# Group 0 tiled by whole batches, its first tile made from the first gather alone, and w1 loaded at once

## The chip, the cores and the metric

The kernel runs on one core of a Trainium2 chip. The core has a matrix engine (PE, with its weight loads PEld), a vector engine (DVE), a scalar engine (ACT), GpSimd (POOL) and a queue engine (SP) that here issues DMAs; 16 DMA engines move data between HBM and the on-chip memory SBUF. The metric is the device time of one launch in microseconds, the median of several runs.

## The reference

For 512 rows of a batch, 32 ids each pick a row of 32 numbers from 32 tables. Two layers of a compressed interaction network follow, then a small dense tower.

```python
e = jnp.stack([tbl_0[ids[:, 0]], ..., tbl_31[ids[:, 31]]], axis=1)   # 512 x 32 fields x 32
x0 = prev = e
for W in (filter_0, filter_1):                                       # 1024 x 128, then 4096 x 128
    z = jnp.einsum('bhd,bmd->bhmd', x0, prev).reshape(b, h * m, d)
    prev = jax.nn.relu(jnp.einsum('bpd,pn->bnd', z, W[0]))
    outs.append(prev)
z = jnp.sum(jnp.concatenate(outs, axis=1), axis=-1)                  # sum over d
h = jnp.concatenate([z, dense_ctx], axis=1)
h = jnp.maximum(h @ W_top1 + b_top1, 0.0)
h = jnp.maximum(h @ W_top2 + b_top2, 0.0)
y = h @ W_top3
```

## The kernel before

**Tiling.** The 512 x 32 pairs of batch and d are 16,384 columns: 32 groups of 512 columns (16 batches), each group four tiles of 128 (u = 0 to 3). Layer 0 is made for a whole group. Layer 1 is made tile by tile: the tile's c (128 maps of layer 0 by 128 columns) is the stationary operand, and w1 streams past it in eight banks (k = 0 to 7) of four fields, 512 columns each. Each bank is three matmuls, because numbers are split into a high and a low part (`hi` by `w_hi`, `hi` by `w_lo`, `lo` by `w_hi`; lines 915, 916 and 923), and goes to one of six PSUM banks in a ring, so bank k of a tile reuses the place of the one six banks earlier.

**Behind PE.** ACT multiplies banks 0, 1, 3, 5, 6 by the embedding value (L571), DVE banks 2, 4, 7 and adds them to ACT's (L740), POOL folds one half of the tile's products onto the other (L441), and DVE reduces the rest in two halves (L752). Those engines follow PE in an order written out by hand: functions are called at places (u, k) of the loop in `body`.

**Groups.** Three gathers of embeddings are made ahead. POOL issues four gathers per group (one for each four batches). SP writes the gathered rows to a scratch in HBM (`send`) and reads them back as pairs (`fetch`), POOL multiplies them to z (L431), ACT rounds z (L532), and PE's layer 0 of the next group stands between layer-1 banks at the places `Z_USED_AT`.

**The start**, which the change rewrites. Group 0 does not go through the scratch. Its gathered rows are spread over 512 columns (each block of 32 rows copied to its own quarter, zeros elsewhere: `spread_hi` on ACT, `spread_lo` on DVE), and six pairs of matmuls with 0/1 matrices ("picks", L940 and L943) put the rows that belong together under each other, one result for the first factor and five for the second (`PICK_ORDER` 4, 0, 1, 2, 3). ACT copies the first factor out, DVE multiplies: first for the first tile alone, then for the other three (`multiply_others`). PE makes layer 0 of the first tile, then layer 1 of the first tile with layer 0 of the other three (`other_tiles`) between its banks; layer 1 of the tile u = 1 comes behind that. Group 0 is laid out like all others: its columns run over (batch, o, d within o), and tile o takes 8 of the 32 values of d of all 16 batches. So every tile needs all four gathers.

PE runs warm-up matmuls on zeros until its inputs arrive (`WARM_UP`). POOL issues twelve gathers (three groups), the last four behind `first_c_hi`, and then takes the low parts of w1's banks 6 and 7. DVE takes the low parts of the others (`rest_w1`), ACT rounds all (`round_w1`). SP loads w1 in four parts of 512 KB: the first at once, the second and third when group 0's gathers are in, the fourth behind the sending of group 1:

```python
            filters(0)
            ...
            sp.wait_ge(gathered[0], 16 * TG)
            for n in range(1, W1_LOADS - 1):
                filters(n)
            ...
            send(Group(0, 1))
            filters(W1_LOADS - 1)
            fetch(Group(0, 1))
```

## Time and profile before

| | us |
|---|---|
| median of 3 runs (834.12 to 834.23) | 834.16 |
| the profiled execution | 833.78 |
| its span, first to last instruction | 832.0 |
| PE busy in it | 825.9 |
| DVE, ACT, POOL busy | 789.3, 795.8, 731.0 |
| granted clock of PE | 1.00 throughout |

The profile is one execution. A row of a timeline gives the start and the length from it in us, the engine, the line of the kernel, the operation, what it writes and reads with shapes, and how many were merged into the row; in brackets stands the idle time of the engine before it and what ended that. Matmuls are pipelined and their ends are modelled: a 512-column matmul lasts 0.39 in the rows, but the next one starts 0.23 later. An fp32 matmul counts as two.

### The profile page before, as it was taken

How to read it: one execution, taken by the hardware profiler on the slowest of the kernel's cores; microseconds unless marked ns; L12 is line 12 of the kernel's file. 1: busy time of each engine (PE TensorE's matmuls, PEld its weight loads, DVE VectorE, ACT ScalarE, POOL GpSimd, SP SyncE). 2: the span in 40 equal slices, each digit the busy share in tenths (PEclk: the TensorE clock that was granted, in tenths of full speed). 3: DMA queues.
4: the chain of work that ended last, by engine and by line, in shares of the span. 5: the costliest groups of instructions: out<-in, count | busy, mean ns of one | idle time of the engine just before them, and what ended most of it. 6: DMA issues, size and time to landing. Idle time of an engine off the chain costs nothing.

```text
span 832.0 us, 15690 instructions
## 1 busy us (share of the span) xinstructions
PE 825.9 (99%) x3627; PEld 677.7 (81%) x3627; DVE 789.3 (95%) x2061; ACT 795.8 (96%) x2808; POOL 731.0 (88%) x550
## 2 busy tenths in 40 slices
PE   8999999999999999999999999999999999999999
PEld 6688888888888888888888888888888888888887
DVE  7799999999999999999999999999999999999996
ACT  4799999999999999999999999999999999999995
POOL 5898999989999999999999999999999999999860
PEclk9999999999999999999999999999999999999999
DMA  5541222221233221132331132221122222122000
GB/s 149 180 143 32 66 81 85 86 85 36 63 82 84 84 86 47 51 85 82 84 87 49 48 87 80 84 86 55 43 87 80 86 85 68 33 83 78 1 13 2
DMA packets 62024, 60.91 MB, mean 73 GB/s; under 512 B 26059, under 2 KB 36939, under 8 KB 61934
## 3 DMA queue, kind: packets, MB, share of 16 engines
q1 hardware_dynamic: 57838, 57.80, 23.4%
q0 software_dynamic: 4096, 2.11, 1.6%
q8 instruction: 32, 0.52, 0.3%
q14 instruction: 58, 0.48, 0.2%
HBM read 55.51 MB, written 4.31 MB: 72 GB/s over the span
## 4 chain that ended last, share of the span: by engine, by line
PE 97%; DMA 1%; POOL 1%; issue 0%; SPq 0%; DVE 0%; ACT 0%
PE ps_y L915 28%; PE ps_y L923 28%; PE ps_y L916 28%; PE ps_c L898 3%; PE ps_c L897 3%; PE ps_c L896 3%; POOL gat L452 1%; PE ps_c L894 1%; DMA w_raw<-w 1%; PE ps_c L885 0%; DMA gat<-table,rows 0%; PE ps_y L1019 0%; DMA ids_and_bounds_sb<-ids_and_bounds 0%; POOL w_lo L459 0%; PE ps_y L1021 0%
## 5 line engine op out<-in xcount | busy, mean ns | idle before, releaser
L571 ACT ACTIVATE prod<-ps_y,es 128x128 f32<-128x128 f32 x2560 | 754.1, 647 | 15.8 <-PE ps_y L923 15.6
L740 DVE SCALAR_TENSOR_TENSOR prod<-ps_y,es,prod 128x128 f32<-128x128 f32 x1536 | 422.6, 340 | 28.7 <-PE ps_y L923 26.4
L915 PE MATMUL ps_y<-w_hi,c_both 128*128 128x512 f32 x1024 | 402.8, 393 | 1.0 <-POOL w_lo L459 1.0
L923 PE MATMUL ps_y<-w_hi,c_both 128*128 128x512 f32 x1024 | 398.8, 390 | 0.0
L916 PE MATMUL ps_y<-w_lo,c_both 128*128 128x512 f32 x1024 | 398.6, 389 | 0.0
L441 POOL TENSOR_TENSOR prod<-prod 128x768 f32<-128x768 f32 x128 | 247.1, 1931 | 45.9 <-DVE prod L740 34.2
L752 DVE TENSOR_REDUCE csum<-prod 128x64 f32<-128x896 f32 x256 | 276.5, 1081 | 0.1
L916 PEld LDWEIGHTS ps_y<-w_lo,c_both 128*128 128x128 f32 x1024 | 192.4, 188 | 43.2 <-issue 1.0
L915 PEld LDWEIGHTS ps_y<-w_hi,c_both 128*128 128x128 f32 x1024 | 192.5, 188 | 42.9 <-issue 2.8
L923 PEld LDWEIGHTS ps_y<-w_hi,c_both 128*128 128x128 f32 x1024 | 192.2, 188 | 41.4
L431 POOL TENSOR_TENSOR z<-first,second 128x512 f32<-128x512 f32 x155 | 199.7, 1299 | 0.1
L419 POOL TENSOR_TENSOR z_lo<-z,z_hi 128x512 fp32r<-128x512 f32 x121 | 155.9, 1298 | 1.0 <-issue 1.0
L410 POOL DMA_INDIRECT gat<-table,rows_now x116 | 110.6, 953 | 31.3 <-issue 28.2
L532 ACT ACTIVATE z_hi<-z 128x512 fp32r<-128x512 f32 x120 | 109.3, 911 | 0.0
L898 PE MATMUL ps_c<-z_lo,w_hi 128*128 128x512 f32 x120 | 48.8, 407 | 0.0
L896 PE MATMUL ps_c<-z_hi,w_hi 128*128 128x512 f32 x120 | 46.6, 388 | 0.0
L897 PE MATMUL ps_c<-z_hi,w_lo 128*128 128x512 f32 x120 | 46.6, 388 | 0.0
L725 DVE TENSOR_REDUCE h<-c_both 128x16 f32<-128x1024 f32 x32 | 38.7, 1208 | 0.0
L532 ACT ACTIVATE z_hi<-z,copy_sb 128x512 fp32r<-128x512 f32 x31 | 35.8, 1154 | 0.0
L555 ACT ACTIVATE c_parts<-csum 128x512 f32<-128x512 f32 x31 | 33.8, 1090 | 0.0
L897 PEld LDWEIGHTS ps_c<-z_hi,w_lo 128*128 128x128 f32 x120 | 22.5, 188 | 4.7
L896 PEld LDWEIGHTS ps_c<-z_hi,w_hi 128*128 128x128 f32 x120 | 22.5, 188 | 4.7
(122 smaller groups left out, 295.7 us busy)
## 6 DMA issues: line engine op xcount, KB each, us to landing
second<-et_scratch SPq DMA_DIRECT2D x155, 256.0 KB, 4.8
first<-et_scratch SPq DMA_DIRECT2D x31, 256.0 KB, 3.2
et_scratch<-gat SPq DMA_DIRECT2D x62, 64.0 KB
w_raw<-w SPq DMA_DIRECT2D x4, 512.0 KB, 4.7
h_scratch<-h_sums SPq DMA_DIRECT2D x120, 2.0 KB
gat<-table,rows_now POOLq DMA_INDIRECT x116, 2.4
wt_sb<-wt SPq DMA_DIRECT2D x2, 512.0 KB
rows_now<-rows SPq DMA_DIRECT2D x29, 2.0 KB, 1.7
```

The lines of the kernel that those rows point to most:

```text
L410: pool.indirect_dma_start(out=gat[:, g.r, u * D:(u + 1) * D], out_offset=None, in_=table, in_offset=bass.IndirectOffsetOnAxis(ap=rows_now[ ...
L419: nc.gpsimd.tensor_tensor(z_lo[:, k, :], z[:, k, :], z_hi[:, k, :].bitcast(F32), ALU.subtract).then_inc(z_lo_ready, LOWS if unsplit(g) else 1)
L431: nc.gpsimd.tensor_tensor(z[:, k, :], first[:, :], second[:, k, :], ALU.mult).then_inc(z_ready, 1)
L441: nc.gpsimd.tensor_tensor(high, high, low, ALU.add).then_inc(folded, 1)
L532: nc.scalar.activation(z_hi[:, k, :], z[:, k, :], ACT.Copy, scale=copy_sb[:, 0:1] if k == LASTK else 1.0).then_inc(z_hi_ready, splits_at_o ...
L571: last = nc.scalar.activation(prod[:, buffer_of(g, u), place // 2, :, place % 2], ps_y[:, bank_of(g, u, k), j * N:(j + 1) * N], ACT.Copy, ...
L740: last = nc.vector.scalar_tensor_tensor(out=summed, in0=ps_y[:, bank_of(g, u, k), j * N:(j + 1) * N], scalar=es[:, g.r, u, h:h + 1], in1=s ...
L752: nc.vector.tensor_reduce(csum[:, g.r, maps, u], prod[:, buffer_of(g, u), fields_folded(g, u) // 2:SCALED // 2, maps, :].rearrange("p a n ...
L896: nc.tensor.matmul(ps_c[:, :], w0_hi[:, k, :], high, start=(k == 0), stop=False)
L915: nc.tensor.matmul(out, hi, w_hi, start=True, stop=False)
L916: nc.tensor.matmul(out, hi, w_lo, start=False, stop=False)
L923: nc.tensor.matmul(out, lo, w_hi, start=False, stop=True).then_inc(y_ready, 1)
```

## The change

Group 0 gets its own column order: tile u holds four whole batches by 32 of d, and these are the rows that gather u brings. The first gather has a semaphore of its own (`first_gathered`), and the first tile is made from it alone.

- The spread is made by DVE, by multiplying the gathered rows with a 0/1 table (`own_block`, four more columns of `copy_sb`), so two memsets of 512 columns and the eight small copies go. The first tile's six picks are single fp32 matmuls of 128 columns on unrounded data; those of the other tiles are twelve matmuls of 384 columns and stand between the layer-1 banks of the first tile (`pick_others`), in two free banks and `ps_h1`.
- The other tiles' layer 0 comes between banks 4 to 7 of the first tile, not 0 to 5.
- SP issues all four w1 loads at once. POOL takes the low parts of three banks, not two, and issues the last four of its first twelve gathers behind them. The warm-up is 22 matmuls instead of 32.
- The rest of w0 moves to (1, 0). Layer 0 of group 1 moves one bank later, its Relu and rest two banks. The sum of group 0's layer 1 over d is made tile by tile in group 1 (`sum_first`: four transposes and four reductions in place of a reduction, a transpose and a reduction).

```diff
-WARM_UP = 32
+WARM_UP = 22
 PICK_ORDER = (4, 0, 1, 2, 3)
+PICK_LOADS = ("first",) + PICK_ORDER
+OTHER_PICKS = {"first": 4, 4: 5, 0: None, 1: 4, 2: 5, 3: None}
+LATE_LO = 3
...
-            filters(0)
+            for n in range(W1_LOADS):
+                filters(n)
-            sp.wait_ge(gathered[0], 16 * TG)
-            for n in range(1, W1_LOADS - 1):
-                filters(n)
...
-            filters(W1_LOADS - 1)
...
+                ).then_inc(gathered[n // TG] if n else first_gathered, 16)
+            pool.wait_ge(rows_step, 4)
+            for n in range(2 * TG):
+                gather_first(n)
+            for k in range(NK - LATE_LO, NK):
                                         ALU.subtract).then_inc(w1_last_lo, 1)
+            for n in range(2 * TG, FIRST_ROWS):
+                gather_first(n)
...
-            round_w1((0, 1))
-            act.wait_ge(spread_zeroed, 2)
-            act.wait_ge(gathered[0], 16 * TG)
-            for q in range(BT):
-                at = slice(q * F, (q + 1) * F)
-                nc.scalar.activation(spread_hi[at, q * P:(q + 1) * P], gat[at, 0, :], ACT.Copy).then_inc(spread_hi_ready, 1)
+            round_w1((0,))
             act.wait_ge(picked, 1)
-            nc.scalar.activation(first_picked, ps_y[:, PICKS["first"], :], ACT.Copy).then_inc(first_copied, 1)
-            round_z(slice(0, 1), first_z_hi, 1)
-            round_w1((2, 3))
+            round_z(FIRST_TILE, first_z_hi, 1)
+            round_w1((1,))
             act.wait_ge(l0_first, 1)
             rectify_first(FIRST_TILE, ps_h1, first_c_hi)
-            round_w1((4, 5))
+            round_w1((2,))
+            act.wait_ge(spread_ready, 2)
+            nc.scalar.activation(spread_hi, spread[:, OTHER_TILES], ACT.Copy).then_inc(spread_hi_ready, 1)
+            round_w1((3, 4))
+            nc.scalar.activation(first_picked[:, OTHER_TILES], picks_of_others("first"), ACT.Copy).then_inc(first_copied, 1)
+            round_w1((5,))
             def body(g, number):
                 more = number is None or number + 1 < GROUPS
                 for u in range(TG):
                     for k in range(NK):
+                        if number == 0 and (u, k) == (0, 1):
+                            act.wait_ge(z_ready, 1)
+                            round_z(OTHER_TILES, z_hi_ready, SPLIT)
+                            round_w1((6,))
                         if number == 0 and (u, k) == (0, 3):
-                        if number == 0 and (u, k) == (0, 5):
+                            round_w1((7,))
+                        if number == 0 and (u, k) == (0, 6):
...
-            nc.vector.tensor_tensor(w0_lo[:, 0:LASTK, :], w0_sum[:, 0:LASTK, :], w0_hi[:, 0:LASTK, :].bitcast(F32),
-                                    ALU.subtract).then_inc(w_ready, 1)
+            def spread_first():
+                dve.wait_ge(first_gathered, 16)
+                shape = [P, BT, D]
+                nc.vector.tensor_tensor(spread[:, FIRST_TILE].rearrange("p (q d) -> p q d", d=D),
+                                        gat[:, 0, 0:D].unsqueeze(1).broadcast_to(shape), own_block.unsqueeze(2).broadcast_to(shape),
+                                        ALU.mult).then_inc(spread_ready, 1)
+                nc.vector.transpose(es[:, 0, 0, :], gat[:, 0, 0:D]).then_inc(first_es, 1)
+                dve.wait_ge(gathered[0], rows_gathered(Group(0, 0)))
+                shape = [P, TG - 1, BT, D]
+                nc.vector.tensor_tensor(spread[:, OTHER_TILES].rearrange("p (u q d) -> p u q d", q=BT, d=D),
+                                        gat[:, 0, D:TG * D].rearrange("p (u d) -> p u d", d=D).unsqueeze(2).broadcast_to(shape),
+                                        own_block.unsqueeze(1).unsqueeze(3).broadcast_to(shape), ALU.mult).then_inc(spread_ready, 1)
...
+                dve.wait_ge(picked, len(PICK_LOADS) + 2 + PICK_ORDER.index(k))
+                multiply_picked(k, OTHER_TILES, picks_of_others(k), z_ready)
...
+            def sum_first():
+                dve.wait_ge(parts_rectified, 1)
+                dve.wait_ge(h1_written[0], 16 * BT)
+                for u in range(TG):
+                    if u > 0:
+                    nc.vector.transpose(c1_turned[:, :], c1_parts[:, :, u]).then_inc(c1_ready if u == TG - 1 else first_turned, 1)
+                    nc.vector.tensor_reduce(h1_sums[:, 0, :].rearrange("p (j b) -> p j b", b=BT)[:, :, u],
+                                            c1_turned[:, :].rearrange("p (j d) -> p j d", d=D), AX.X,
+                                            ALU.add).then_inc(h1_summed if u == TG - 1 else first_turned, 1)
...
-            rest_w1(0)
-            rest_w1(1)
-            for q in range(BT):
-                dve.wait_ge(spread_hi_ready, q + 1)
+            spread_first()
+                multiply_picked(k, FIRST_TILE, ps_y[:, PICKS[k], FIRST_TILE], first_z)
+            rest_z(FIRST_TILE, first_z_lo, 1)
+            rest_w1(0)
+            rest_first(FIRST_TILE, ps_h1, first_c_hi, first_c_lo)
+            rest_w1(1)
+            spread_others()
+            rest_w1(2)
+            dve.wait_ge(spread_hi_ready, 1)
+            nc.vector.tensor_tensor(spread_lo, spread[:, OTHER_TILES], spread_hi.bitcast(F32), ALU.subtract).then_inc(spread_lo_ready, 1)
+            rest_w1(3)
+            turn_others()
+            dve.wait_ge(first_copied, 2)
+            multiply_others(LASTK)
             multiply_others(0)
-            turn(Group(0, 0))
-            rest_first(FIRST_TILE, ps_h1, first_c_hi, first_c_lo)
+            rest_w1(4)
             multiply_others(1)
-            rest_w1(2)
-            multiply_others(2)
-            rest_w1(3)
-            multiply_others(3)
-            multiply_others(LASTK)
                         if number == 0 and (u, k) == (0, 2):
-                            rest_w1(4)
-                        if number == 0 and (u, k) == (0, 4):
-                            rest_w1(5)
+                            multiply_others(2)
+                            multiply_others(3)
                             dve.wait_ge(z_hi_ready, SPLIT)
-                            dve.wait_ge(z_ready, KP)
-                            rest_z(slice(1, TG), z_lo_ready, LOWS)
+                            dve.wait_ge(z_ready, 1)
+                            rest_z(OTHER_TILES, z_lo_ready, LOWS)
+                        if number == 0 and (u, k) == (1, 0):
+                            rest_w0()
...
+                        if more and (u, k) == ((3, 5) if number == 0 else (3, 3)):
...
+                    if k < NK - LATE_LO:
+                        pe.wait_ge(w1_last_lo, k + 1 + LATE_LO - NK)
+                    if k in (4, 5):
+                        pe.wait_ge(z_ready, k - 1)
...
-            pe.wait_ge(picks_ready, 1)
-            pe.wait_ge(spread_hi_ready, BT)
                 table_of, shift = {"first": (1, 0), LASTK: (1, P // 2)}.get(load) or (0, 16 * load)
-                out, picks_of = ps_y[:, PICKS[load], :], picks_r[:, table_of, shift:shift + P]
-                nc.tensor.matmul(out, picks_of, spread_hi, start=True, stop=False)
+            pe.wait_ge(spread_ready, 1)
+            for load in PICK_LOADS:
+                table_of, at = picks_at(load)
+                nc.tensor.matmul(ps_y[:, PICKS[load], FIRST_TILE], picks_sb[:, table_of, at], spread[:, FIRST_TILE],
+                                 start=True, stop=True).then_inc(picked, 1)
+            def pick_others(load):
-                nc.tensor.matmul(out, picks_of, spread_lo, start=False, stop=True).then_inc(picked, 1)
-            def first_layer0(k, tiles, out):
+                    pe.wait_ge(picks_ready, 1)
+                    pe.wait_ge(spread_hi_ready, 1)
+                    pe.wait_ge(spread_lo_ready, 1)
+                if load == 1:
+                    pe.wait_ge(first_copied, 2)
+                if load in (2, 3):
+                    pe.wait_ge(z_ready, load - 1)
+                table_of, at = picks_at(load)
+                nc.tensor.matmul(picks_of_others(load), picks_r[:, table_of, at], spread_hi, start=True, stop=False)
+                nc.tensor.matmul(picks_of_others(load), picks_r[:, table_of, at], spread_lo, start=False, stop=True).then_inc(picked, 1)
-                return first_layer0(k, slice(1, TG), ps_c[:, OTHER_TILES])
-            pe.wait_ge(w_ready, 2)
+                if k < LASTK:
+                    pe.wait_ge(z_ready, PICK_ORDER.index(k) + 1)
+                    return nc.tensor.matmul(ps_c[:, OTHER_TILES], w0_sum[:, k, :], z[:, k, OTHER_TILES], start=(k == 0), stop=False)
...
-            other_tiles(0)
-            Z_USED_AT_FIRST = ((1, 6), (2, 1), (2, 4), (2, 6), (3, 0))
+            Z_USED_AT_FIRST = ((1, 7), (2, 2), (2, 5), (2, 7), (3, 1))
...
-                        if number == 0 and u == 0 and 1 <= k < LASTK:
-                            other_tiles(k)
-                        if (number, u, k) == (0, 0, LASTK):
+                        if number == 0 and u == 0 and k in (2, 3):
+                            for load in PICK_LOADS[3 * k - 6:3 * k - 3]:
+                                pick_others(load)
+                        if number == 0 and u == 0 and k in (4, 5):
+                            other_tiles(k - 4)
+                        if number == 0 and u == 0 and k == 6:
+                            other_tiles(2)
+                            other_tiles(3)
                             other_tiles(LASTK).then_inc(l0_done, 1)
```

At its start PE had, from the last pick through layer 0 of the first tile to layer 1:

```order
L940 MATMUL ps_y<-z_hi,picks_r 128x512
L943 MATMUL ps_y<-z_lo,picks_r 128x512
L949 MATMUL ps_h<-z,w_sum 128x128 x4
L951 MATMUL ps_h<-z_lo,w_lo 128x128
L949 MATMUL ps_c<-z,w_sum 128x384
L915 MATMUL ps_y<-w_hi,c_both 128x512
L916 MATMUL ps_y<-w_lo,c_both 128x512
```

It now has, from the warm-up on to the third bank and the first picks of the other tiles:

```order
L1001 MATMUL ps_y<-z_lo 128x512 x22
L1011 MATMUL ps_y<-csum,picks_sb 128x128 x6
L1032 MATMUL ps_h<-z,w_sum 128x128 x4
L1034 MATMUL ps_h<-z_lo,w_lo 128x128
L982 MATMUL ps_y<-w_hi,c_both 128x512
L983 MATMUL ps_y<-w_lo,c_both 128x512
L982 MATMUL ps_y<-w_hi,c_both 128x512
L983 MATMUL ps_y<-w_lo,c_both 128x512
L990 MATMUL ps_y<-w_hi,c_both 128x512 x2
L982 MATMUL ps_y<-w_hi,c_both 128x512
L983 MATMUL ps_y<-w_lo,c_both 128x512
L990 MATMUL ps_y<-w_hi,c_both 128x512
L1025 MATMUL ps_y<-z_hi,picks_r 128x384
L1026 MATMUL ps_y<-z_lo,picks_r 128x384
```

The picks of the first tile are narrow, and those of the others have moved behind the third layer-1 bank.

SP's queue at the start, before (`w_raw<-w` are the w1 loads, `et_scratch<-gat` the sending of group 1):

```order
L318 DMA copy_sb<-copy_of 128x2
L319 DMA picks_sb<-picks 128x384
L314 DMA w_raw<-w 128x1024 x3
L340 DMA et_scratch<-gat 4x32x128 x2
L314 DMA w_raw<-w 128x1024
L357 DMA first<-et_scratch 128x1x512
```

and now:

```order
L331 DMA copy_sb<-copy_of 128x6
L332 DMA picks_sb<-picks 128x384
L327 DMA w_raw<-w 128x1024 x4
L351 DMA et_scratch<-gat 4x32x128 x2
L368 DMA first<-et_scratch 128x1x512
```

The fourth load has moved ahead of the sending, and the wait for group 0's gathers that stood within the first three is gone.

POOL's start before (`gat<-table` are gathers, `w_lo` the low parts of w1, `z` the products of group 1, `prod` the fold):

```order
L452 DMA gat<-table,rows 128x32 x12
L459 ISA
L459 TENSOR_TENSOR w_lo<-w_raw,w_hi 128x512 x2
L431 TENSOR_TENSOR z<-first,second 128x512 x3
L441 TENSOR_TENSOR prod<-prod 128x768
```

and now:

```order
L460 DMA gat<-table,rows 128x32 x8
L471 ISA
L471 TENSOR_TENSOR w_lo<-w_raw,w_hi 128x512 x3
L460 DMA gat<-table,rows 128x32 x4
L441 TENSOR_TENSOR z<-first,second 128x512 x3
L451 TENSOR_TENSOR prod<-prod 128x768
```

Four gathers have moved behind the low parts of w1, which are three.

## Rows read from the trace of the kernel before

**Rows 1.** The page: busy time and share of each engine.

```profile
PE 825.9 (99%) x3627; PEld 677.7 (81%) x3627; DVE 789.3 (95%) x2061; ACT 795.8 (96%) x2808; POOL 731.0 (88%) x550
```

**Rows 2.** Timeline of PE, the first 27 us: start, length, what.

```profile
1.45 9.00 PE L934 MATMUL ps_y<-z_lo 128*128 128x512 f32 x32 [1.45 <-DVE z_lo L655]
...
12.08 0.47 PE L940 MATMUL ps_y<-z_hi,picks_r 128*128 128x512 f32 x1 [1.63 <-ACT z_hi L590]
...
14.98 1.05 PE L949 MATMUL ps_h<-z,w_sum 128*128 128x128 f32 x8
...
15.79 0.31 PE L951 MATMUL ps_h<-z_lo,w_lo 128*128 128x128 f32 x1
...
16.64 0.69 PE L915 MATMUL ps_y<-w_hi,c_both 128*128 128x512 f32 x1
...
18.32 0.81 PE L949 MATMUL ps_c<-z,w_sum 128*128 128x384 f32 x2
...
19.20 0.40 PE L916 MATMUL ps_y<-w_lo,c_both 128*128 128x512 f32 x1
...
25.59 0.47 PE L915 MATMUL ps_y<-w_hi,c_both 128*128 128x512 f32 x1 [0.32 <-POOL w_lo L459]
...
26.36 0.40 PE L915 MATMUL ps_y<-w_hi,c_both 128*128 128x512 f32 x1
```

**Rows 3.** DMA to landing of gathers issued at 4.02, 5.48-9.45, 10.70-13.20, 37.97-41.74.

```profile
DMA to landing us min/median/max: 3.7/3.7/3.7
...
DMA to landing us min/median/max: 2.3/2.5/3.0
...
DMA to landing us min/median/max: 3.3/4.1/5.1
...
DMA to landing us min/median/max: 6.0/6.2/6.5
```

**Rows 4.** Timeline of DVE, and its busy time in one group's 25.4 us.

```profile
7.11 0.69 DVE L678 TENSOR_TENSOR w_lo<-w_sum,w_hi 128x512 fp32r<-128x512 f32 x1
...
7.72 0.35 DVE L681 SCALAR_TENSOR_TENSOR w_lo<-w_hi,copy_sb,w_sum 128x128 fp32r<-128x128 f32 x1
...
15.38 0.28 DVE L701 TENSOR_TENSOR z_lo<-z,z_hi 128x128 fp32r<-128x128 f32 x1
...
32.12 1.07 DVE L752 TENSOR_REDUCE csum<-prod 128x64 f32<-128x896 f32 x1
...
51.70:77.10 25.40, 25.40 (x114) 20.92 (x113) 24.41 (x64) 24.89 (x91) 23.11 (x18) 1.00 0.24 71
```

**Rows 5.** Timeline of ACT, the Relu of the first tile.

```profile
16.13 0.28 ACT L542 ACTIVATE c_both<-ps_h 128x128 fp32r<-128x128 f32 x1 [0.26 <-PE ps_h L951]
```

**Rows 6.** SP's issues; landing of the first w1 load; GB/s (last column), 14 to 15.

```profile
3.09 8.29 SPq L314 DMA_DIRECT2D w_raw<-w  x3
...
34.41 3.18 SPq L359 DMA_DIRECT2D second<-et_scratch  x5
...
39.19 0.39 SPq L371 DMA_DIRECT2D wt_sb<-wt  x1
...
DMA to landing us min/median/max: 5.0/5.0/5.0
...
14.00:15.00 1.00, 1.00 (x6) 0.78 (x6) 0.65 (x3) 0.55 (x2) 0.14 (x1) 1.00 1.00 406
```

**Rows 7.** Timeline of POOL: a gather, w1's low parts, products, the first fold.

```profile
19.17 0.94 POOL L452 DMA_INDIRECT gat<-table,rows  x1 [0.30 <-issue]
...
22.93 2.52 POOL L459 TENSOR_TENSOR w_lo<-w_raw,w_hi 128x512 fp32r<-128x512 f32 x2 [1.56 <-ACT w_hi L580]
...
25.60 3.80 POOL L431 TENSOR_TENSOR z<-first,second 128x512 f32<-128x512 f32 x3
...
29.36 1.85 POOL L441 TENSOR_TENSOR prod<-prod 128x768 f32<-128x768 f32 x1
```

**Rows 8.** Warm-up matmuls between 3 and 4 us: ns min/median/max, first and last start.

```profile
L934 PE MATMUL ps_y<-z_lo x4: 628/628/628, 2.5 to 3.8; 128*128 128x512 f32 x4
```

More of the change, by code:

```diff
@@ L564, in scale @@
                 if k == ACT_BANKS[u][0]:
-                    if u == 0:
+                    if u == 0 and g.times(1) == 0:
+                        act.wait_ge(first_es, 1)
+                    elif u == (1 if g.times(1) == 0 else 0):
                         act.wait_ge(es_ready, g.times(1, 1))
@@ L622, in body @@
                             rectify_end(u - 2)
-                        if more and (u, k) == (3, 1):
+                        if more and (u, k) == ((3, 3) if number == 0 else (3, 1)):
                             rectify_hi(g.plus(1))
@@ L732, in scale @@
                 if k == DVE_BANKS[u][0]:
-                    if u == 0:
+                    if u == 0 and g.times(1) == 0:
+                        dve.wait_ge(first_es, 1)
+                    elif u == (1 if g.times(1) == 0 else 0):
                         dve.wait_ge(es_ready, g.times(1, 1))
```

106 lines of the change are left out of this document (59 added, 47 removed).

## The prediction

> **What bounds the kernel now.** I read the page's busy line first: PE is busy for 825.9 us, 99% of the span [rows 1]. So a change pays only if PE starts its steady stream earlier, does less work, or waits less. I then read PE's timeline over the first 30 us [rows 2]. It has four pieces to see: the 32 warm-up matmuls from 1.45 (9.00 us), a gap of 1.6 until the first pick at 12.08, the twelve picks until layer 0 of the first tile at 14.98, and the first layer-1 matmul at 16.64. The second tile of group 0 (u = 1) starts at 26.36, and from there PE has no more gaps worth naming. That makes 26.36 the mark of this study. Everything behind it is a rigid block of PE work which the change hardly touches. What counts is the time at which u = 1 starts, and whether PE stays fed behind it.
>
> **What the change removes ahead of the mark.** Before, the picks wait for all four gathers; now one is enough. Call the landing of the first gather T0. In the trace of before it is issued at 4.02 and lands 3.7 later, at 7.7 [rows 3]. DVE has finished the part of w0 that the first tile needs by then: w_lo of 128 columns at 7.72 comes 0.6 earlier with the row of 0.69 ahead of it moved away, so it ends at 7.4 [rows 4]. The warm-up is no obstacle either: ten matmuls fewer at 0.23 each (the spacing, as between 25.59 and 26.36) end it at 10.45 − 2.3 = 8.2 [rows 2].
>
> **The chain from T0 to the first layer-1 matmul**, all from the durations of the nearest kind of instruction [rows 2, 4, 5]. The spread product (128x128 on DVE) 0.28, with the hand-over the first pick starts at T0+0.36. A 128-column fp32 matmul takes PE 0.27 (1.05 for four); the first result stands at T0+0.8, ACT's copy takes 0.28, to T0+1.1. The five products on DVE follow the picks at 0.27 each, the last ending at T0+2.5, its rest at T0+2.7 (0.28). The last layer-0 matmul adds 0.31 and its start-up (T0+3.1), the Relu 0.28 (T0+3.4). Layer 1 starts at T0+3.45. ACT's round of the last product and the w1 rests lie beside this.
>
> **From there to u = 1.** PE has 24 layer-1 matmuls at 0.23 = 5.5; 12 picks of 384 columns, at three quarters of that, 0.17 each = 2.0; four fp32 matmuls of 384 columns at 0.65 (18.32 to 19.20 less one of 0.23) = 2.6; the low one 0.2. That is 10.3. The picks of three tiles and one of the fp32 products are new in this stretch: before they stood ahead of 16.64. Waits that I find by laying the DVE rows in their new order: bank 1 waits 0.4 for its w1 rest, which now stands behind the rest of c (0.29 + 0.69 after the Relu); 0.2 ahead of bank 2, behind the spread of the others; 0.5 ahead of bank 4, which waits for the third product; 0.1 ahead of u = 1. Sum 1.2. So u = 1 starts at T0 + 3.45 + 10.3 + 1.2 = T0 + 15.0 (rounded). The waits for the last w1 rests (0.32 ahead of the last bank is one of them [rows 2]) go, because w1 is all in by then. Against 26.36, **the gain is 11.4 − T0**. All steps hang on T0 alone (ACT and DVE reach their w1 work only behind the first tile), so a late T0 moves the whole chain.
>
> **T0 is the term that decides.** Now SP issues all four w1 loads at 3.09, 3.5, 4.0 and 4.4, around the issue of the first gather (4.02 to 5.17). The trace shows what a gather does behind such a backlog. With little ahead of them gathers land 2.3 to 3.0 after their issue. The three issued from 10.70, just when the second and third w1 load were issued, took up to 5.1 [rows 3]; the four issued from 37.97, with a fetch (five loads of it from 34.41) and the tower's weights (39.19) queued on SP [rows 6], took 6.0 to 6.5 [rows 3]. So gathers stand behind what SP has queued, even those parts issued a little later. By these rows T0 is: 7.7 if the three added loads do not matter; 4.02 + 5.1 = 9.1 by the w1 row; 4.02 + 6.5 = 10.5 by the deepest backlog; and at most the end of all w1, which is the first load's landing 3.09 + 5.0 = 8.1 plus three times 512 KB at 406 GB/s (1.3 each), 12.0 [rows 6]. The backlog at 4.4 is 2.1 MB of w1 and the tail of w0 and the picks, more than in either row, so I take the upper of the observed ones, **T0 = 10.5**. That is nearly when the fourth gather landed before: the first gather alone is then no earlier, and what is left of the gain is that DVE and PE do less work ahead of the first tile.
>
> A page speaks against this reading. The Trainium skill, page "DMA: Bandwidth & Descriptors", section "Queues, rings and completion order", says that each DMA engine serves the queues in turn, packet by packet, so a gather would slip in between the w1 packets. By that alone T0 stays near 7.7 and the gain is 3.7, by my row it is 0.9. The gathers of 6.0 to 6.5 do not bear the page out.
>
> **Behind the mark.** PE's slots for layer 0 of group 1 are one bank later, its inputs are not late: the gathers of group 1 no longer meet w1 and land by 13.2 + 2.4 = 15.6 instead of 16.5, so SP sends 1 us earlier. But GpSimd now does three w1 rests (1.28 each [rows 7]), the last one behind ACT's last round (ACT reaches it after two scaled banks, T0+11.4), and four gathers after them (1.25 apart [rows 7]): T0+12.7, T0+17.7. Then three products, 3.80, and the first fold, 1.85: T0+23.4. DVE would reduce the first tile 5.8 after the mark (32.12 − 26.36 [rows 2, 4]), at T0+20.8. It stands still for 2.6, where it did not before. Queued behind that wait is its scaling of bank (1,7), which ends at T0+23.4+1.1+1.1 = T0+25.6; PE wants that ring bank at (2,5), 10.7 after the mark, T0+25.7. So the six banks just cover it. In group 1 the new sum of the first group costs DVE four times (0.29 + 0.27) against 1.23 before, 1.0 more, while DVE has only 1.0 per group to catch up with (busy 24.41 of 25.40 [rows 4]). I charge 0.3, with bounds 0 (cover holds) and 1.5 (both lags add). Moving w0's rest to (1,0) costs 0.69 of DVE in a gap, nothing on PE; the later Relu and rest of c at (3,3) and (3,5) keep 0.6 of margin; copy_sb is 16 bytes wider per row, nothing.
>
> **Sum.** The profiled execution took 833.78 (span 832.0 and 1.8 around it); the median is 834.16, 0.38 above. 833.78 − (11.4 − 10.5) + 0.3 = 833.2 profiled, **833.6 as a median**. About 0.2% (1.7 us) is what a measurement of this kernel can tell from no change, so this is "the same".
>
> **Rivals.**
> - *The first gather comes at 9.1* (the w1 row's own 5.1). For it: the same loads, issued in the same way. Against: twice their number. 834.16 − 2.3 + 0.3 = 832.2, just over the bound: faster. Chance 0.20.
> - *The gather slips through* (the page's rule), T0 = 7.7: 834.16 − 3.7 + 0.3 = 830.8. For it: in the trace of before the first gather lands at 7.7 although one w1 load of 8.1 was in flight, so not wholly behind it. Against: rows 3. Chance 0.14.
> - *Slower by the clock.* PE has nothing from the end of the warm-up at 8.2 until T0+0.36; in before the gap was 1.6 us and the matmuls after it ran at the full clock. If T0 is 11.6, near the end of w1, the gap is 3.8, and the granted clock may fall from 2.4 to 1.2 GHz as it stood at the start. The page "TensorE: Matmul & The Clock Gate" of the Trainium skill, section "What's actually happening", says that idling brings the lower clock back; no row here shows a fall. Price: warm-up matmuls lasted 628 ns at the start, instead of some 390, until about 4.6 [rows 8], 3.1 us at half rate, 1.6 lost. 834.16 + 0.2 + 0.3 + 1.6 = 836.3. It decides from T0 of about 11. Chance 0.12.
> - *The fold comes too late* and PE does wait: the upper bound of 1.5 instead of 0.3 with T0 = 10.5, 834.8. Chance 0.06.
>
> **How the numbers follow.** The forecast (T0 between 9.8 and 11.9, full clock) has 0.48 and 833.6, its own range 832.7 to 835.2. The 0.8 range must take in the 9.1 case, most of the early case and the late fold, but not the clock case: 830.7 to 835.4. Faster by over 0.2% (below 832.5): 0.14 + 0.16 of the 9.1 case + 0.02 = 0.32. Slower (above 835.8): 0.12 + 0.01 = 0.13. Within: 0.55.
>
> **What would show it.** The landing time of the first gather from its issue at 4.02: 6.5 (mine), 5.1, 3.7 or over 7.5. The first pick at T0+0.4, layer 1 at T0+3.45, u = 1 at T0+15.0. The granted clock between 8 and 15 below 1.00, or picks at twice 0.27, would be the clock rival. On DVE, an idle time of some 2.6 before the first reduce, waiting for the fold. I am wrong if u = 1 minus T0 is not 15.0, which would be a mis-sized wait of the four between banks, or if PE shows gaps behind the mark of more than 0.3.

## The result

The changed kernel is slower. Six runs of it took 842.85 to 851.94 us, median 843.78; six of the kernel before, beside them, 833.85 to 834.36, median 834.19. The ratio is 1.0133, 95% interval 1.0112 to 1.0155, so 1.1% to 1.6% slower. The forecast was 833.6, with a range of 830.7 to 835.4. The profiled execution is the longest of the six, 851.94 (span 850.1); the other five lie between 842.85 and 844.86. One stall in it is missing from a second profile of the same kernel (843.69 us, below), and so most likely from those five.

### The profile page after: what moved, and what is told of

Same layout as the page of the kernel before. It is cut to its first block, busy times and chain, and to the rows that moved or that the text cites. A ratio compares the mean times of both kernels' runs of the same rounds, so it can differ in the third digit from the quotient of the medians.

```text
span 850.1 us, 15700 instructions
## 1 busy us (share of the span) xinstructions
PE 832.1 (98%) x3629; PEld 681.3 (80%) x3629; DVE 803.9 (95%) x2063; ACT 796.5 (94%) x2806; POOL 731.5 (86%) x551
## 4 chain that ended last, share of the span: by engine, by line
PE 94%; DVE 3%; issue 1%; DMA 1%; ACT 0%; DVEq 0%; ACTq 0%
PE ps_y L982 27%; PE ps_y L990 27%; PE ps_y L983 27%; PE ps_c L963 3%; PE ps_c L961 3%; PE ps_c L962 3%; DVE prod L789 1%; DMA gat<-table,rows 1%; PE ps_c L959 1%; DVE z_lo L759 1%; PE ps_c L1040 0%; PE ps_c L949 0%; ACT prod L587 0%; PE ps_y L1011 0%; PE ps_y L1108 0%
## 5 line engine op out<-in xcount | busy, mean ns | idle before, releaser
L963 PEld LDWEIGHTS ps_c<-z_lo,w_hi 128*128 128x128 f32 x120 | 22.6, 188 | 4.7
```

The source lines that it names most:

```text
L963: nc.tensor.matmul(ps_c[:, :], w0_hi[:, k, :], low, start=False, stop=False)
```

## The profile of the changed kernel

On the page, PE is busy 832.1 us where [rows 1] have 825.9, in a span 18.1 us longer. So 6.2 us stand in PE's busy time, nearly all as matmuls at a lower clock (the same instructions in e10 below, where the clock stays up, are busy for 826.5 us); the other 11.9 are standing still.

```profile
PE 832.1 (98%) x3629; PEld 681.3 (80%) x3629; DVE 803.9 (95%) x2063; ACT 796.5 (94%) x2806; POOL 731.5 (86%) x551
```

Timeline of PE (start, length, what, idle time before it and what ended it), the lines that answer to [rows 2]:

```profile
12.13 2.15 PE L1011 MATMUL ps_y<-csum,picks_sb 128*128 128x128 f32 x12 [3.20 <-DVE csum L707]
...
15.65 0.45 PE L1034 MATMUL ps_h<-z_lo,w_lo 128*128 128x128 f32 x1
16.47 0.50 PE L982 MATMUL ps_y<-w_hi,c_both 128*128 128x512 f32 x1 [0.37 <-ACT c_both L556]
...
17.39 0.50 PE L982 MATMUL ps_y<-w_hi,c_both 128*128 128x512 f32 x1 [0.19 <-DVE w_lo L838]
...
23.37 0.48 PE L982 MATMUL ps_y<-w_hi,c_both 128*128 128x512 f32 x1 [1.13 <-DVE z L731]
...
29.03 0.50 PE L982 MATMUL ps_y<-w_hi,c_both 128*128 128x512 f32 x1
...
40.42 0.77 PE L982 MATMUL ps_y<-w_hi,c_both 128*128 128x512 f32 x1 [4.64 <-DVE prod L789]
...
242.63 0.76 PE L961 MATMUL ps_c<-z_hi,w_hi 128*128 128x512 f32 x1 [4.83 <-DVE z_lo L759]
```

The picks start at 12.13, no earlier than before (12.08). Layer 1 starts at 16.47 (before 16.64). The mark, the start of u = 1, is at 29.03 instead of 26.36: 2.67 late. And there are two holes that the forecast does not know, of 4.64 and 4.83 us.

The same stretches by window (length, then busy time of PE, PEld, DVE, ACT, POOL, then the granted clock, the share of the DMA engines and GB/s):

```profile
8.20:11.90 3.70, 0.74 (x4) 0.27 (x2) 0.20 (x1) 0.69 (x2) 2.79 (x4) 1.00 1.00 390
11.90:14.00 2.10, 1.87 (x12) 1.90 (x13) 1.08 (x6) 0.95 (x3) 1.79 (x2) 0.75 0.36 115
14.00:16.40 2.40, 2.10 (x11) 1.91 (x9) 1.27 (x4) 0.51 (x3) 0.05 (x1) 0.51 0.04 7
...
36.00:40.40 4.40, 0.00 (x0) 0.01 (x1) 4.40 (x6) 0.00 (x0) 2.68 (x3) 0.98 0.03 6
40.40:43.50 3.10, 3.08 (x7) 2.50 (x8) 3.10 (x7) 1.30 (x5) 0.93 (x1) 0.50 0.93 285
```

Read the clock column: behind the gap of 3.20 us the granted clock fell to the lower level (0.51 is 1.2 GHz), and again at the end of the hole at 36 to 40. In that hole DVE is busy all 4.40 us. With what, its own timeline and GpSimd's tell:

```profile
11.70 0.29 DVE L707 TENSOR_TENSOR csum<-gat,copy_sb 128x128 f32<-128x128 f32 x1 [3.98 <-DMA gat<-table,rows]
...
30.52 8.72 DVE L700 TENSOR_TENSOR w_lo<-w_sum,w_hi 128x512 fp32r<-128x512 f32 x1
39.16 1.11 DVE L789 SCALAR_TENSOR_TENSOR prod<-ps_y,es,prod 128x128 f32<-128x128 f32 x4
...
235.96 6.53 DVE L759 TENSOR_TENSOR z_lo<-z,z_hi 128x512 fp32r<-128x512 f32 x1
```

```profile
29.74 0.95 POOL L460 DMA_INDIRECT gat<-table,rows  x1 [0.30 <-issue]
30.69 3.79 POOL L441 TENSOR_TENSOR z<-first,second 128x512 f32<-128x512 f32 x3
34.44 1.81 POOL L451 TENSOR_TENSOR prod<-prod 128x768 f32<-128x768 f32 x1
36.21 2.47 POOL L441 TENSOR_TENSOR z<-first,second 128x512 f32<-128x512 f32 x2
42.57 1.83 POOL L451 TENSOR_TENSOR prod<-prod 128x768 f32<-128x768 f32 x1 [3.90 <-DVE prod L789]
```

The rest of w0 (L700) is the instruction that took 0.69 at 7.11 before [rows 4]. Moved to (1,0) it takes 8.72. It ends at 39.24, 0.6 after GpSimd's sixth instruction in a row (38.68), and GpSimd then waits for what DVE has queued behind L700. So DVE was not working: it was kept out for as long as GpSimd ran without a pause. At 235.96 the same befalls L759, the rest of z, which takes 0.68 in the other groups. I call this a shut-out. The page "SBUF — State Buffer" of the Trainium skill, section "Who interferes with whom", says that a DVE instruction with two SBUF inputs and a GpSimd instruction that reads SBUF exclude each other, and the one issued second waits until the first has finished. The trace agrees on the pair, and that the wait outlasts five or six GpSimd instructions (6.5 to 8.7 us) goes beyond what the Trainium skill says there. L700 also began before the first product did (30.52 against 30.69, while a gather, L460, still ran) and was passed over all the same. The shut-out at 235.96 comes in a group in which GpSimd is late for another reason: it had waited 0.80 us for a transfer at 221.59, its only such wait in the run.

Where each later loss arises is read best from one DVE instruction that runs once in each group, the sum of h0 (`h<-c_both`, 1.21 us; before at 29.96, 57.61, 82.62, ... 796.89). Its start, minus that of before:

```
kernel                   group 0     1      2      3   ...  7      8      9   ...  31
changed, first profile    10.24   9.36  10.75  10.38     10.37  17.51  18.17     18.19
changed, second profile    9.64   8.91  10.29   9.89      9.88   9.89   9.89      9.90
```

The second profile (e18_after_again, 843.69 us) has the first shut-out and not the one at 236. That is the usual run. Its 9.9 us are 2.1 at the mark (28.42), 7.6 in the first shut-out, 0.7 of which come back, and 1.0 between groups 1 and 3.

## Experiments

Every experiment was timed beside the kernel before, whose medians were 833.8 to 834.1; ratios are to those runs.

**Take away the first victim, or let GpSimd wait for it; and stage the loads.** e1 moves the rest of w0 back, ahead of all that waits (not its exact old place, but before the first products of DVE):

```
+            spread_first()
+            rest_w0()
...
-                        if number == 0 and (u, k) == (1, 0):
-                            rest_w0()
```

e2 leaves it at (1,0) and makes GpSimd wait for it:

```
+                    if number == 0 and u == 0:
+                        pool.wait_ge(w_ready, 2)
```

e3 takes back only the loads at once, and e4 is e1 and e3 together:

```
-            for n in range(W1_LOADS):
-                filters(n)
+            filters(0)
...
+            sp.wait_ge(first_gathered, 16)
+            for n in range(1, W1_LOADS):
+                filters(n)
```

> The changed kernel with the rest of w0 (the DVE subtraction of 8.72 us) moved from (1, 0) to the start, behind the spread of the first tile, where DVE stands idle. Theory A (DVE was shut out while GpSimd ran one product after the other, and PE ran dry behind that): the instruction takes 0.7 us, PE's gap of 4.6 at 35.8 and the low clock behind it go, and the time falls by 6 to 7 from 843.4, to about 837. What is left against before is the late mark (about +2.7). Theory B (the wait is that of the late fold, whatever DVE does before it): a DVE gap of 2 to 3 us ahead of the first reduce takes its place, the time falls by less than 3, to over 840.

> The changed kernel with one wait more: GpSimd waits for the rest of w0 before its first product of group 1. The rest of w0 stays at (1, 0). Theory A: with GpSimd standing still the same instruction at the same place takes 0.7 to 1 us, GpSimd loses about 1 us once, and the time is about 837 as in the run with the rest moved away. Theory B (the place on DVE, or the late fold, is what costs): no change, 843, or more, since GpSimd is later still.

> The changed kernel with SP waiting for the first gather before it issues the second to fourth w1 load. First gather: theory A (a gather stands behind everything that SP queued): lands 3.7 after its issue, at 7.7 instead of 11.7, PE's gap after the warm-up is below 1 us, its clock stays at the full level and u = 1 starts at 7.7 + 15 to 15.5 = about 23. Theory B (the lateness has another cause, such as GpSimd's own issue): it stays at 11. The rest of w0 at (1, 0) is still there, so the gap on PE stays about as it is: 843.4 - 6 = 837 by A, 843 by B.

> Both: the rest of w0 at the start and the w1 loads behind the first gather. If the two causes are separate and together all of the loss, u = 1 starts at about 23, PE has no gap behind it, and the time is 834.2 - (26.4 - 23) = about 831, below the kernel before. If the late fold counts as well (DVE held until GpSimd has folded the first tile), PE shows a gap of 0.3 to 1.5 behind the mark and the time is 831.5 to 832.5.

Measured: e1 845.34 (ratio 1.0132, 1.0111 to 1.0152; one of its four runs took 861.21 and is not in the ratio), e2 846.43 (1.0144), e3 844.36 (1.0113), e4 845.49 (1.0123). None gave anything back; in e3 the rest of w0 took 8.75 as before. In e2, on the same chip and at the same place, the rest of w0 does take its 0.68, so it is GpSimd's chain that keeps DVE out. DVE and GpSimd in e2:

```profile
31.16 0.68 DVE L702 TENSOR_TENSOR w_lo<-w_sum,w_hi 128x512 fp32r<-128x512 f32 x1
...
31.92 3.80 POOL L441 TENSOR_TENSOR z<-first,second 128x512 f32<-128x512 f32 x3 [0.61 <-DVE w_lo L702]
```

But in e1, e2 and e4 the shut-out moved on to L759 (L761), at 54.3, 55.0 and 55.4, with 7.0, 7.6 and 6.9 us. DVE and GpSimd in e19_w0_early_again, which is e1 on another chip (845.26), and then PE in e1:

```profile
54.05 7.07 DVE L759 TENSOR_TENSOR z_lo<-z,z_hi 128x512 fp32r<-128x512 f32 x1
...
52.57 2.54 POOL L441 TENSOR_TENSOR z<-first,second 128x512 f32<-128x512 f32 x2
55.08 1.81 POOL L451 TENSOR_TENSOR prod<-prod 128x768 f32<-128x768 f32 x1
56.86 1.26 POOL L441 TENSOR_TENSOR z<-first,second 128x512 f32<-128x512 f32 x1
58.09 2.48 POOL L429 TENSOR_TENSOR z_lo<-z,z_hi 128x512 fp32r<-128x512 f32 x2
```

```profile
61.51 0.77 PE L960 MATMUL ps_c<-z_hi,w_hi 128*128 128x512 f32 x1 [5.12 <-DVE z_lo L759]
```

So my first theory, that the place of w0's rest is the fault, fell. What stays is a GpSimd that never pauses. In an ordinary group the fold waits for DVE's scaling just when DVE starts its rest of z. GpSimd and DVE in the kernel before:

```profile
51.62 2.17 POOL L441 TENSOR_TENSOR prod<-prod 128x768 f32<-128x768 f32 x1 [0.24 <-DVE prod L740]
...
51.40 0.68 DVE L719 TENSOR_TENSOR z_lo<-z,z_hi 128x512 fp32r<-128x512 f32 x1
```

In 29 of its 30 groups with such a rest there is a pause like this, of 0.24 us in the first and 0.5 to 0.9 in the others, and the rest takes 0.68. In the thirtieth (672.71) there is none, and the rest takes 0.82. My reading is that the pause is what lets DVE in. Here GpSimd starts its first products at 30.69, 1.7 after the mark; before at 25.60 [rows 7], 0.8 ahead of it. A late GpSimd finds every wait met.

**Each suspect alone, in the kernel before, and the pause put back.** e5 is the kernel before with all four w1 loads at once. e6 is the kernel before with w0's rest at (1,0). e8 is the changed kernel with GpSimd's old order. The edit of e5:

```
-            filters(0)
+            for n in range(W1_LOADS):
+                filters(n)
...
-            sp.wait_ge(gathered[0], 16 * TG)
-            for n in range(1, W1_LOADS - 1):
-                filters(n)
...
-            filters(W1_LOADS - 1)
```

of e6:

```
+                        if number == 0 and (u, k) == (1, 0):
+                            rest_w0()
...
-            pe.wait_ge(w_ready, 2)
+            pe.wait_ge(w_ready, 1)
```

of e8:

```
-LATE_LO = 3
+LATE_LO = 2
...
+            pool.wait_ge(first_c_hi, 1)
+            for n in range(2 * TG, FIRST_ROWS):
+                gather_first(n)
             for k in range(NK - LATE_LO, NK):
...
                             rest_z(OTHER_TILES, z_lo_ready, LOWS)
+                            rest_w1(5)
```

and e10, which is e1 with one wait more:

```
+                    if u == 1 and (number is None or 0 < number < GROUPS - 1):
+                        wait(pool, z_lo0_ready, g.plus(1).times(1, 1 - UNSPLIT))
                     if u > 0 and folds_late:
                         fold(g, u - 1)
```

> The kernel before with all four w1 loads issued at once and nothing else changed. Theory (the loads delay the gathers, and that is all they do): the fourth gather of group 0 lands near 13.4 as in the changed kernel instead of 10.5, so the start of u = 1 moves from 26.4 to about 28.5-29.3; GpSimd and VectorE move together, every VectorE rest keeps its 0.7 us, and the time is 836.0 to 837.5. Rival (the loads alone also bring the 7 to 9 us shut-outs of VectorE): one rest of over 5 us and 840 or more.

> The kernel before with the rest of w0 moved to (1,0), as in the changed kernel, and nothing else. Theory (an operation of VectorE with two SBUF inputs that meets a chain of back-to-back GpSimd instructions waits for the end of the chain): GpSimd runs without a pause from 25.6 to 35.5 there, so the rest, reached near 27.5, takes 7 to 9 us, PE stands still for about 5, and the time is 839 to 842. Rival (only a GpSimd that is late by the three w1 rests makes it): the rest takes 0.7 to 1.5 us, 834.0 to 834.8.

> The changed kernel with the order of GpSimd from before: gathers 8 to 11 ahead of its w1 rests (behind the first c), two w1 rests on it and the third on VectorE; the rest of w0 stays at (1,0). Chain theory: the chain now starts near 26 and ends near 35.5, the rest of w0 reached near 30 takes 5 to 6 us, PE loses 2 to 4 us, 838 to 841, and no rest at line 759 is long. Rival (lateness of GpSimd alone is the cause): no operation over 1.5 us, 836 to 837.

> The changed kernel with the rest of w0 early (as in e1_w0_early), and GpSimd waits ahead of its first fold in groups 1 to 30 until VectorE has the rest of z of lag 0 behind it. Chain theory: GpSimd stands still for up to 1 us near 55, the rest of z takes at most 1.7 us, no VectorE operation over 2 us anywhere, PE has no gap over 1.5 us behind 29; the time is 836.3 to 837.5, which is the late start of u = 1 alone. Rival (a late GpSimd hands the shut-out to the next operation with two SBUF inputs, whatever waits): another operation over 5 us and 841 or more.

Measured: e10 835.92 (1.0028, 1.0016 to 1.0041), and 836.98 (1.0032) when repeated as e23_protect_again. The shut-outs are gone, and with them some 8 to 9 us. DVE and GpSimd in e10:

```profile
52.03 1.56 DVE L761 TENSOR_TENSOR z_lo<-z,z_hi 128x512 fp32r<-128x512 f32 x1
...
50.49 2.54 POOL L441 TENSOR_TENSOR z<-first,second 128x512 f32<-128x512 f32 x2
53.67 1.85 POOL L451 TENSOR_TENSOR prod<-prod 128x768 f32<-128x768 f32 x1 [0.64 <-DVE z_lo L761]
```

DVE still waits for the product that runs (1.56 instead of 0.68), but then gets in, because the fold now waits 0.64 for it. DVE had to wait 1.01 us for the running product here; in e1 and e19, without the pause, 1.03 and 1.07 us, and there it was shut out. The chain theory holds for the cure and not for my forecast of e6, which was 839 to 842: it took 833.81 (0.9997, 0.9987 to 1.0006).

```profile
28.28 0.90 DVE L680 TENSOR_TENSOR w_lo<-w_sum,w_hi 128x512 fp32r<-128x512 f32 x1
...
26.08 4.26 POOL L431 TENSOR_TENSOR z<-first,second 128x512 f32<-128x512 f32 x3
30.30 1.85 POOL L441 TENSOR_TENSOR prod<-prod 128x768 f32<-128x768 f32 x1
```

Here the same instruction met the same three products, and got in after 0.35, between the second and the third; the three took 4.26 instead of 3.80, so this time GpSimd waited. In e8 it took 1.17. Being beside a chain is thus not enough.

e5 took 838.40 (1.0055, 1.0038 to 1.0071), above the 836.0 to 837.5 that I expected, without any shut-out. Its whole 4.4 us stand at group 0 already. The picks start at 14.63 instead of 12.08 and at the lower clock, and the twelve of them take 5.3 instead of 2.9:

```profile
14.63 0.77 PE L937 MATMUL ps_y<-z_hi,picks_r 128*128 128x512 f32 x1 [3.32 <-ACT z_hi L587]
```

So the loads at once harm by themselves, by the late gathers and by the clock that falls in the gap. e8 took 838.81 (1.0055), 838 to 841 expected. It has no shut-out either, but my third rest of w1 on DVE stood 2.2 us in PE's way and the clock fell for it, so it tells little of its own.

**The loads staged, the sums spread, more warm-up, each on top of e10.** e14 adds the staging of e3. e15 puts the four transposes and sums of the first group, which stand in one piece at (2,4) of group 1, at (2,4), (2,7), (3,2) and (3,5). e16 has both. e17 is e10 with 32 warm-up matmuls (`WARM_UP = 32`). The edit of e15 (`sum_first` now does one of the four pieces):

```
-                        if (u, k) == (2, 4) and number == 1:
-                            sum_first()
+                        if number == 1 and (u, k) in SUM_FIRST_AT:
+                            sum_first(SUM_FIRST_AT.index((u, k)))
...
+            SUM_FIRST_AT = ((2, 4), (2, 7), (3, 2), (3, 5))
```

> The kernel of e10_protect, with the second to fourth w1 load issued only when the first gather has landed (as in e3_w1_staged). Backlog theory: the first gather lands near 8.7 instead of 10.7, the first pick runs at 9.1 to 9.5, and if PE then works at its normal pace the start of u = 1 comes 1 to 2 us before the 26.4 of e10_protect: 834.3 to 835.3. Rival (whatever held PE in e3_w1_staged and e4_both, where results of PE arrived 2.0 to 2.8 us behind the matmul's place, belongs to staged loads): layer 0 of the first tile again ends near 15.5 and the time is 836 to 837.5.

> The kernel of e10_protect, with the four transposes and sums of group 0 (line 818 on, 2.9 us in one piece on VectorE at (2,4) of group 1) at (2,4), (2,7), (3,2) and (3,5) instead. Theory (the piece in one holds back the scaling that PE waits for: the groups stand 1.0 us later from group 2 on, and PE waits 0.34 at 70.43): the offset of the groups against the kernel before falls from 1.7 to 0.7-1.2, 835.0 to 835.4. Rival (the work itself, 1.6 us more than before, is what costs, wherever it stands): unchanged, 835.9.

> Both edits, e14_protect_staged and e15_sum_spread, in one kernel. If both gains are real and add up: 833.2 to 834.5, level with or better than the kernel before. If the staging brings nothing: 835.0 to 835.5.

> The kernel of e10_protect with 32 warm-up matmuls instead of 22, as in the kernel before: PE is then busy until the first gather lands, at no cost for the first pick if that is at 11.1. If the low clock after the gap of 1.7 to 3.2 us (granted 0.5 from 13.0 to 16.4 in the changed kernel, absent in the profile of e10_protect) takes part in the median: 834.9 to 835.6. If it does not: 835.8 to 836.1, and below 0.5 us of the 7.9 us between the changed kernel and e10_protect was the clock of the first tile.

Measured: e14 833.58 (0.9985, 0.9959 to 1.0010), e15 835.79 (1.0023, 1.0013 to 1.0033), e16 833.08 (0.9985, 0.9969 to 1.0001), e17 835.74 (1.0018, 1.0009 to 1.0028). The offsets of the sum of h0:

```
kernel                   group 0     1      2      3   ...  31
e10_protect                0.32   1.02   2.02   1.64      1.65
e15_sum_spread             0.90   1.59   2.16   1.73      1.74
e14_protect_staged        -1.94  -1.24  -0.28  -0.65     -0.64
e16_spread_staged         -1.80  -1.11  -0.47  -0.84     -0.82
```

What is left in e10 is 0.3 at the mark, 0.7 in group 1 and 0.6 in the sums. The staging is worth 2.3 us (1.64 to -0.65). In e16 the early first tile arrives 1.8 us ahead of the kernel before, and behind it 0.7 goes in group 1 (DVE waits for a product, and the fold for it) and 0.3 in the sums. In e14 the sums in one piece cost 0.6 (from -1.24 to -0.65), in e10 0.6. Spreading them gives back 0.3 to 0.5 in the traces; the median of e15 does not show it against e10, since its first tile came 0.6 later, by chance as far as I can see. The extra warm-up does not move the median (835.74 against 835.92), but no run of it is above 836.11, where e10 has two of 837.1 with a clock of 0.997 to 0.998. (Beside e14 to e17 three of the 30 runs of the kernel before took 840.8 to 842.2, and the ratios take them in; by medians e14 and e16 stand at 0.9995 and 0.9989.)

**The same kernels on other chips.** The first four runs had been made on another chip than those up to e17, so I ran the changed kernel and e1 again, and two more: e20 is the changed kernel with gathers 8 to 10 ahead of the three rests, e21 is e16 with that edit. Then e10 and e16 once more, as e23 and e24.

```
-            for n in range(2 * TG):
+            for n in range(FIRST_ROWS - 1):
                 gather_first(n)
             for k in range(NK - LATE_LO, NK):
...
-            for n in range(2 * TG, FIRST_ROWS):
-                gather_first(n)
+            gather_first(FIRST_ROWS - 1)
```

> The changed kernel once more, unaltered, beside the others. If the shut-outs are the kernel's own: about 843.8, a rest of w0 of 6 to 9 us near 30.5, PE empty for over 4 us near 36-40. If they belong to the chip of the first runs: 836 to 837.

> The kernel of e1_w0_early once more. If the shut-out at line 759 near 54 is the kernel's own: 843 to 845.5. If it belongs to the chip of the first runs: 835.5 to 836.5, and the wait in e10_protect did nothing.

> The changed kernel with gathers 8 to 10 ahead of the three rests of w1 on GpSimd (in the time in which it waits for ScalarE anyway), one gather behind them; the rest of w0 stays at (1,0). The first products then start near 27 instead of 30.7. Theory (GpSimd is late because of these gathers, and being late is what exposes the VectorE rests): no VectorE operation over 2 us, no gap of PE over 1.5 us behind the start of u = 1, 835.5 to 837. Rival (the rest of w0 beside any GpSimd chain is enough): it meets the products at 30.5 and takes 5 us or more, 840 or more.

> The kernel of e16_spread_staged (w0 early, w1 loads staged, the sums spread, GpSimd waiting for the rest of z) with gathers 8 to 10 ahead of the rests of w1. The offset that the wait of GpSimd left in group 1 (0.7 us between the first two groups of e16_spread_staged) should go, since GpSimd is no longer late: 832.2 to 832.9, against 833.1 of e16_spread_staged and 834.0 before. If the gathers delay the rests or the w1 loads instead, PE waits for its banks 5 to 7: 833.5 to 834.5.

> The kernel of e10_protect once more. If the shut-outs are cured by the wait whatever the chip: no VectorE operation over 2 us, 836 to 838 (835.9 before, and up to 2 more if PE's first results come late). If the cure was the chip: 843 or more.

> The kernel of e16_spread_staged once more. If PE's first results come in time: 833.1 as before, the first tile's layer 0 ending at 11.4. If they are held until the first eight gathers have landed: its layer 0 counts at 15.4, the start of u = 1 moves to 28 or later, and the time is 836 to 838.

Measured: e18 845.01 (1.0133), e19 845.26 (1.0135), e20 842.79 (1.0103), e21 838.07 (1.0046), e23 836.98 (1.0032, 1.0020 to 1.0044), e24 833.24 (0.9993, 0.9984 to 1.0002). e18 and e19 have the shut-outs again, so that two chips of the experiments show them; e10 and e23 have none, on two others. The kernel of e10 was never run on a chip that had shown a shut-out, so it is not shown that the chip has no part. (e21, on the chip of e19, has the pause and no shut-out, but its GpSimd had already been idle for 0.18 us when the first rest of z came.) Within one chip the evidence is e2 against e3, 0.68 against 8.75 us for the same instruction. The first profile of the changed kernel has shut-outs in a complete trace, so the gaps in the records of e18 and e19, described below, are not what makes them.

e20 and e21 met something else. e20 has no shut-out (w0's rest 1.19, every rest of z 0.7), yet it is slow from the first tile on, 7.5 us at group 0. ACT and PE in e20:

```profile
19.85 0.28 ACT L555 ACTIVATE c_both<-ps_h 128x128 fp32r<-128x128 f32 x1 [6.20 <-remote]
```

```profile
14.55 0.33 PE L1033 MATMUL ps_h<-z_lo,w_lo 128*128 128x128 f32 x1
20.18 0.80 PE L981 MATMUL ps_y<-w_hi,c_both 128*128 128x512 f32 x1 [5.29 <-ACT c_both L555]
```

The last layer-0 matmul is placed at 14.55, but ACT learns of its result only at 19.85. That is 4.96 us behind the end of the matmul's row, where the traces of the other chips show 0.04. In e2, e3 and e4 the lag was 1.3, 2.8 and 2.0 us, in e21 3.4; it uses up what staging gains in e3 and e4, while e14 has none of it. It stands only in the traces of two of the four chips that the experiments ran on, those in which a fifth of the DMA completions is not recorded either. Whether the gathers in flight hold PE, or the recording does, I could not settle; the landings of the gathers are among what these traces lack. Since GpSimd was idle in e20 while PE stood (1.68 us ahead of its first product), e20 does not show by itself that the gathers behind the rests are what made GpSimd late.

## Why the prediction was wrong

- *T0 = 10.5.* Too early: 11.67 in the profile (issued 4.06, 7.6 us), 10.5 to 11.3 in the other profiles with all loads at once that record it. The row I leaned on, gathers behind a deep backlog, was the right one, and the bound "all of w1 first" was nearer than the row of 6.5. The page "DMA: Bandwidth & Descriptors" of the Trainium skill, section "Queues, rings and completion order", has each DMA engine serve the queues in turn, packet by packet. What the forecast drew from it, a gather that slips through in 3.7 us, did not come. With the loads staged the same gather takes 4.3 to 4.7 us (e14, e24).
- *Layer 1 at T0 + 3.45.* Right at the full clock: in e10 the gather lands at 10.66 and layer 1 starts at 14.11, 3.45 later. In the profile it took 4.80, since the clock had fallen. The clock rival (chance 0.12, from T0 of about 11, 1.6 us) was right in its mechanism and nearly in its price, 1.35. Its point was right only roughly: the clock fell in e19, where the spread starts at 10.71, and not in e15, where it starts at 11.29. It should have had the chance of the main case. A late T0 and the fallen clock are one case, not two.
- *From layer 1 to the mark, 10.3 of work and 1.2 of waits, 11.5.* It took 12.56, in the profile and in e10, and 12.58 in e24. The waits I had are 1.3 (0.19 and 1.13), with the one at bank 4 more than twice the 0.5 that I gave it. The work was mis-sized: 11.2 instead of 10.3. I had costed matmuls at their closest spacing, 0.23; at several places here they start 0.34 apart.
- These three make the mark: 1.17 + 1.35 + 1.06 = 3.58. My mark was 10.5 + 3.45 + 11.5 = 25.45 before rounding, 0.91 ahead of the old one, and 3.58 less 0.91 is the 2.67 measured.
- *GpSimd late, DVE idle for 2.6 before the first reduce, PE just covered.* GpSimd was late as worked out: in e10, where the clock stayed up, its products start at 28.32, and T0 + 17.7 is 28.4. DVE waits 1.4 for the fold and PE does not wait at all. But I asked only who waits for GpSimd by semaphore. That is the other half of the failed step: in e1, with w0's rest out of the way, the same late GpSimd costs 7.8 us between groups 0 and 1 at the rest of z, a place that the change does not touch and the forecast does not name.
- *"Moving w0's rest to (1,0) costs 0.69 of DVE in a gap, nothing on PE."* This is the step that failed. It cost 8.72 on DVE and 4.64 of hole on PE, and the groups behind it stand 7.6 us later, the lower clock included. The move alone costs nothing (e6, 833.81); it costs this beside a GpSimd that runs late and without a pause, which the same forecast had worked out. I knew the neighbours of its place by busy time, not by what they share. In the trace of before 29 of 30 rests of z fall in a pause of GpSimd, and the thirtieth got in, so no row there gave the price; it belonged in the sum with an upper bound of a chain's length.
- *The new sum of the first group.* I worked out 1.0 more on DVE (2.2 against 1.23; in e10 the piece takes 2.9) and charged 0.3 for it and the fold together. It cost PE 1.0 in the changed kernel and 0.6 in e10. DVE is 96% busy in a group [rows 4], so most of it was likely to reach PE.
- *The rival that ends slower* was the clock, at 836.3. With everything known but the shut-out, the forecast should have been about 836 to 837, where e10 and e23 stand.

What the change set out to do works on two chips, once its side effects are taken off: e16 and e24, with the loads staged and GpSimd pausing, took 833.08 and 833.24, at ratios of 0.9985 and 0.9993 to the kernel before, whose intervals just include 1. That is level, or a tenth of a per cent better. On the two chips with late results of PE, staging brought nothing (e3, e4 and e21).

## What to carry to other kernels

Before an instruction is moved, look at what the other engines do at its new place, and for DVE's instructions with two SBUF inputs look at GpSimd above all: a pause there, even of 0.2 us, is part of the schedule, and a GpSimd that runs late closes it. Taking one victim away only handed the stall on here; with a wait that restores the pause it was gone. And a load that is issued early is paid by the first small transfer behind it: stage it until the transfer that starts PE has landed.

## What the runs showed of the hardware

- Kept out by GpSimd, DVE stays out over a chain of instructions: 8.72, 8.73, 8.75 us for w0's rest, 6.53 to 7.56 for the rest of z, seen in eight meetings in seven profiles. In six other meetings with the next GpSimd instruction ready, DVE got in behind the one that ran. The time it had to wait for the running one does not decide: 0.17 (a gather, in the three of w0's rest), 0.33 and 0.50 us ended in a shut-out, and so did 0.91, 1.03 and 1.07; 0.23 to 0.26 (three times), 0.35, 0.62 and 0.64 did not. What decides is open. Three of 30 runs of the kernel before took 840.8 to 842.2, at a granted clock of 0.995 to 0.996 as the changed kernel has; its margin may fail at times too, which no profile caught.
- Right behind the first gap of PE after the warm-up (or within it) the granted clock fell to 1.2 GHz where that gap was 2.64, 2.80, 2.92, 3.20 or 3.32 us long, and not where it was 1.63, 1.73, 1.99, 2.00, 2.33, 2.46 or 2.56. The length alone does not decide: later gaps of 2.23 us in e8 and 2.32 in e4 were enough.
- Results of PE counted 1.3 to 5.0 us after the end of their matmul's row in five traces (e2, e3, e4, e20, e21), all of two of the chips; the cause is open.
